# Feed-forward after attention without a barrier: first quarter from on-chip blocks, last head pair by quarters, layer 1 without a wait for stores

## The reference

```python
# layer 0; LN = (x - mean) / sqrt(var + 1e-5) over the 1024 features
x = x + 0.5 * ffn(LN(x))        # w1 (1024->4096), depthwise conv of 3 tokens, silu, w2 (4096->1024)
x = x + attn(LN(x))             # 16 heads of 64, softmax, W_o and bias
x = x + 0.5 * ffn(LN(x))        # the same weights a second time
# layer 1
x = x + 0.5 * moe(x); x = x + linear_attn(x); x = x + 0.5 * moe(x)
def bit_linear(x, w):           # in ffn: activations to int8 per token, weights to -1, 0, 1
    s = 127 / max(|x|, per token); return (round(x * s) / s) @ quant(w).T
```

## Time and profile before

| | us |
|---|---|
| time of the kernel, median of 3 runs | 3168.76 (3165.76 to 3183.69) |
| the profiled execution | 3179.94 |
| its span, first to last instruction of the slowest core (core 4) | 3178.4 |
| spans of the 8 cores | 3155.5 to 3178.4 |
| attention's last head pair | 1752 to 1838 |
| last value product to the first w1 product | 1838 to 1931 |
| first quarter of the second feed-forward | 1931 to 2065 |
| last w2 product to the first weight fusing in layer 1 | 2546 to 2571 |

### The profile page before, as it was taken

One profiled execution on the slowest core, in us unless ns is written; L12 is line 12 of the kernel. 1 busy time (PEld: TensorE's weight loads), 2 busy tenths in 40 slices (PEclk: granted clock), 3 DMA queues, 4 the chain that ended last, 5 costly groups with the idle time before them and its releaser, 6 DMA issues.

```text
span 3178.4 us, 39354 instructions; the slowest of 8 cores (3155.5 to 3178.4 us)
## 1 busy us (share of the span) xinstructions
PE 2623.4 (83%) x11770; PEld 1132.0 (36%) x11770; DVE 2017.5 (63%) x2898; ACT 1685.3 (53%) x1983; POOL 377.9 (12%) x438
## 2 busy tenths in 40 slices
PE   1558788895699999999988846697979879899899
PEld 0223233342233444444433312243434334344334
DVE  5698777763587777777767135877777324444443
ACT  5779666552326666666654725675655223414430
POOL 0000001213200110010010000011111212211310
PEclk6879899997899999999999977898989889999999
DMA  8656432335320321221061051142423550000002
GB/s 259 176 154 201 144 115 81 102 92 143 82 37 14 57 50 18 44 44 31 14 143 34 14 165 53 47 120 72 124 70 92 156 172 1 1 27 27 1 11 70
DMA packets 151756, 259.13 MB, mean 82 GB/s; under 512 B 35904, under 2 KB 71760, under 8 KB 151232
## 3 DMA queue, kind: packets, MB, share of 16 engines
q1 hardware_dynamic: 118832, 199.44, 21.5%
q0 software_dynamic: 32720, 57.17, 8.6%
HBM read 220.70 MB, written 52.56 MB: 86 GB/s over the span
## 4 chain that ended last, share of the span: by engine, by line
PE 64%; DVE 14%; ACT 9%; issue 8%; DMA 4%; POOL 1%; SPq 0%; DVEq 0%; ACTq 0%; POOLq 0%
PE fb L1731 11%; PE fb L1492 9%; PE aups L598 7%; PE mb L2316 7%; PE apps L712 6%; PE asps L693 6%; PE ajps L562 3%; PE mb L2107 2%; DVE amx L609 2%; PE rs L2205 2%; DVE fbig L1542 2%; PE mb L2373 2%; PE asps L657 2%; ACT fbig L1528 1%; PE st L2153 1%
## 5 line engine op out<-in xcount | busy, mean ns | idle before, releaser
L609 DVE TENSOR_REDUCE amx<-aups 128x1 f32<-128x512 f32 x1024 | 663.1, 687 | 213.0 <-PE aups L598 211.4
L702 ACT ACTIVATE aet<-asps 128x1024 bf16<-128x1024 f32 x512 | 523.1, 1024 | 279.6 <-PE asps L693 273.7
L1492 PE MATMUL fb<-shb,fw1r 128*128 128x512 bf16 x2048 | 542.6, 405 | 107.8 <-DVE fbig L1546 76.8
L1731 PE MATMUL fb<-fbig 128*128 128x512 bf16 x2048 | 494.5, 391 | 60.1 <-ACT fbig L1692 29.5
L598 PE MATMUL aups<-ahd 65*128 65x512 bf16 x1024 | 356.7, 386 | 21.2 <-DVE amx L609 8.3
L1492 PEld LDWEIGHTS fb<-shb,fw1r 128*128 128x128 fp8e4 x2048 | 207.5, 103 | 398.1 <-issue 198.9
L712 PE MATMUL apps<-aet,avt 128*65 128x512 bf16 x1024 | 311.6, 385 | 11.4 <-ACT aet L702 8.0
L1731 PEld LDWEIGHTS fb<-fbig 128*128 128x128 fp8e4 x2048 | 203.4, 100 | 320.7 <-issue 96.8
L693 PE MATMUL asps<-ahd 65*128 65x512 bf16 x1024 | 311.3, 387 | 0.0
L1528 ACT ACTIVATE fbig<-fb,cbsb,cw2sb 128x512 f32<-128x512 f32 x256 | 196.1, 769 | 203.0 <-PE fb L1492 189.9
L1542 DVE SCALAR_TENSOR_TENSOR fbig<-fb,cw2sb,fbig 128x511 f32<-128x511 f32 x256 | 191.2, 747 | 166.1 <-ACT fbig L1528 163.6
(11 more groups left out here) (280 smaller groups left out, 3073.7 us busy)
## 6 DMA issues: line engine op xcount, KB each, us to landing
fw1r<-wq SPq DMA_DIRECT2D x224, 128.0 KB, 2.2
fbig<-wq SPq DMA_DIRECT2D x112, 256.0 KB, 2.9
fbig<-w1h SPq DMA_DIRECT2D x32, 512.0 KB, 13.1
fbig<-w2h SPq DMA_DIRECT2D x28, 512.0 KB, 4.2
sha<-x SPq DMA_DIRECT2D x8, 1024.0 KB, 10.5
fw2f<-w2h SPq DMA_DIRECT2D x32, 256.0 KB, 3.8
fbig<-w2h SPq DMA_DIRECT2D x32, 256.0 KB, 3.8
fbig<-x POOLq DMA_DIRECT2D x32, 256.0 KB, 5.2
```

What stands on the lines that cost most here:

```text
L609: lambda e, hh=hh, c=c: e.tensor_reduce(m[:, c:c + 1], ups[hh][:, :], axis=AX.X, op=ALU.max),
L702: ta = A(lambda e: e.activation(et[g % 3][:, :], sps[s][:, :], AF.Exp, scale=0.125), wait=[tp, tk.get(("ef", g % 3))])
L1492: tp = T(lambda e, dc=dc: e.matmul(bank[b][:, :], sl[:, o + dc * 128:o + (dc + 1) * 128], xr[:, dc * 512:(dc + 1) * 512], start=(dc == 0), ...
L1731: tp = T(lambda e, j=j: e.matmul(bank[2 + j][:, :], w2r[s][:, o + j * 128:o + (j + 1) * 128], xi2[:, hc * 512:(hc + 1) * 512], start=(hc = ...
```

## The change

Three parts. (1) The last head pair goes by quarters: head 0 and head 1 of a quarter follow each other, so each quarter of the attention is complete after 16 steps. Its softmax sums no longer go through DRAM: a matmul with a 0/1 matrix `sel` spreads them over 128 partitions, DVE inverts 128x512 and multiplies. The remaining `g_wo` matmuls of pair 7 are done by step 39, and the rest (`g_rest`, pairs 5 to 7 of W_o) is pulled two a step from step 40 on. Stores go by the POOL queue. (2) The second feed-forward has no barrier. It takes quarter 0 where it lies (`xq` = `res[0..7]`), copies the halo columns from the blocks with DVE (`edge_copy`), and pulls the remaining blocks of `g_rest` between its layer norm's steps; the halo's steps lie between those of the quantisation. Reads of x from DRAM wait for the stores of their quarter only. (3) `layer1` waits for the compute engines' own counts instead of the barrier; its loads of x wait for the stores they need. Tiles are allocated in another order, so that none that is written early lies on one still in use.

```diff
@@ attn_l0
-                s_res = [dsem("ares") for _ in range(32)]
+                s_so = [dsem("aso") for _ in range(4)]
+                s_a7 = [[dsem("aa7") for _ in range(2)] for _ in range(2)]
+                s_res = [dsem("ares") for _ in range(16)]
-                def seq(g):
+                def seq(t, g):
+                    if t == 7:
+                        return (g // 8) % 2, g // 16, g % 8
                     return g // 32, (g // 8) % 4, g % 8
+                def last_pair(hh, qb, ta):
+                    base = hh * 64
+                    c = slice(qb * 512, (qb + 1) * 512)
+                    o = ao[:, 7 * T + qb * 512:7 * T + (qb + 1) * 512]
+                    r = rbc[1][:, c]
+                    tk["ao7", qb, hh] = dget(s_a7[qb % 2][hh],
+                        ao[base:base + 64, 7 * T + qb * 512:7 * T + (qb + 1) * 512],
+                        stg[hh][0:64, c],
+                        wait=[ta, tk["xln", 3], tk.get(("n7", qb - 2))])
...
+                    def inv():
+                        for h in range(2):
+                            tp = P(lambda e, h=h: e.matmul(
+                                ups[0][:, :], sel[:, h * 128:(h + 1) * 128],
+                                stg[h][0:65, c], start=(h == 0), stop=(h == 1)),
+                                wait=[tk["st7", qb, h], tk["u0f"],
+                                      tk["sel"]], mark=(h == 1))
+                        tk["u0f"] = tk["r7"] = V(
+                            lambda e: e.reciprocal(r, ups[0][:, :]),
+                            wait=[tp, tk["norm", 5]])
+                    def norm():
+                        tk["n7", qb] = V(lambda e: e.tensor_tensor(o, o, r, ALU.mult),
+                            wait=[tk["r7"], tk["ao7", qb, 0], tk["ao7", qb, 1]])
+                    after(1, inv)
+                    after(3, norm)
+                def g_rest():          # pulled from step 40 on, and in the next stage
...
+                            for ec in range(EA, DC):
+                                tp = wo_mm(rings[i], n, ec, EA, DC - 1, ...)
...
+                            t = V(lambda e, i=i, n=n: e.tensor_tensor(
+                                res[n], rings[i], res[n], ALU.add),
+                                wait=[tp, tk["res", n]])
+                            rt[i] = fin[n] = t
+                            out[qb] = dget(s_so[qb], x_dst[...], res[n],
+                                           wait=[t], eng="gpsimd")
-                        elif t == 7 or g >= 12:
-                            pull(p, 2 if t == 6 else 1)
+                        elif t == 6:
+                            pull(p, 2 if g >= 12 else 0)
+                        elif g < 40:
+                            pull(p, 2 if g % 5 < 2 else 1)
+                        else:
...
+                            pull(rest, 2)
@@ ffn
-            if not first:
-                barrier()
+            if prev is not None:
+                for e in ("scalar", "vector", "gpsimd", "sync"):
+                    em.wait_only(e, [prev["tk"]["pv", 7]])
+                def edge_copy(qb):
+                    t = None
+                    for d0, n, blk in prev["blocks"](qb):
+                        for b, o, c in ((qb, 0, 510), (qb - 1, 2, 0)):
+                            if b not in (0, 1, 2):
+                                continue
+                            t = V(... tensor_copy of two columns of n blocks ...,
+                                  wait=[prev["fin"][8 * qb + 7]])
-                    ln_load(0)
-                    for n in range(NW1):
-                        w1_load(n)
-                    ln_cast(0)
... (all steps of the layer norm, then halo(), then the quantisation)
+                    for n in range(NW1):
+                        w1_load(n)
+                    for k in range(4):
+                        w2_load(k)
+                    ln["dma"] = [fin[7], fin[7]]
+                    ln["held"] = [out[0]]
+                    edge_copy(0)
+                    steps = ln_steps(0)[1:]
+                    for k in range(13):
+                        steps.pop(0)()
+                        for _ in range(3):
+                            next(tail, None)
+                    for _ in tail:
+                        pass
+                    edge_steps = halo()
+                    for k in range(2):
+                        next(edge_steps)
+                    while steps:
+                        steps.pop(0)()
+                        for _ in range(2):
+                            next(edge_steps, None)
@@ layer1
-            barrier()
+            own = [(Sdv, Sdv.c), (Ssc, Ssc.c), (Spe, Spe.c)]
+            for e in ("tensor", "scalar", "vector"):
+                em.wait_only(e, own)
+            for e in ("gpsimd", "sync"):
+                em.wait_only(e, own + [(Sgp, Sgp.c)])
@@ layer1, x_load
-                                 wait=[tk.get(("out", q - 3))])
+                                 wait=[tk.get(("out", q - 3))] +
+                                 stored["x", q])
```

More of the change, by code:

```diff
@@ L478, in attn_l0 @@
                             k65[b][hh][64:65, :], 1.0))
+                V(lambda e: e.memset(sel[:, :], 0.0))
+                V(lambda e: e.memset(sel[64:65, 0:64], 1.0),
+                  wait=[(Sdv, Sdv.c)])
+                tk["sel"] = V(lambda e: e.memset(sel[64:65, 192:256], 1.0))
                 def ln_load(q):
@@ L760, in inv @@
                         if hh == 1:
-                            after(18 if t < 7 else 4, norm)
+                            after(18, norm)
                     def norm():
@@ L769, in norm @@
                                   tk["ao", t, 0], tk["ao", t, 1]])
-                    after(18 if t < 7 else 5, inv)
+                    after(18, inv)
                 EA = 5
@@ L863, in attn_l0 @@
                     tick()
-                    if t == 7:
-                        for _ in p:
-                            pass
                     if t == 5:
@@ L894, in attn_l0 @@
[L894 to L908 removed]
+                while 7 not in fin:
+                    pull(rest)
@@ new lines, in tail, with blocks, f @@
+                def tail():
+                    while later:
+                        pull(rest, 3)
+                        tick()
+                        yield
+                    for _ in rest:
+                        yield
+                def blocks(qb):
+                    def f(ap, n):
+                        return ap.rearrange("p (a b) -> p a b", a=n)
+                    if qb == 0:
+                        return [(0, 8, f(lnb[:, :], 8))]
+                    if qb < 3:
+                        o = (qb - 1) * 8192
+                        return [(0, 8, f(xln[:, o:o + 8192].bitcast(F32),
+                                         8))]
+                    return [(0, 4, f(qkb[:, :].bitcast(F32), 4))] + \
+                        [(4 + 2 * i, 2, f(wqk[i][:, :].bitcast(F32), 2))
+                         for i in range(2)]
@@ L910, in build_program, with ffn @@
+                return dict(tail=tail(), blocks=blocks, fin=fin, out=out,
+                            rt=rt, tk=tk)
         NW1 = 7
         stored = {}
-        def ffn(x_src, x_dst, first):
-            if not first:
-                barrier()
+        def ffn(x_src, x_dst, first, prev=None):
+            if prev is not None:
+                for e in ("scalar", "vector", "gpsimd", "sync"):
+                    em.wait_only(e, [prev["tk"]["pv", 7]])
             with ExitStack() as fctx:
@@ L1018, in ln_load, with made @@
                             .rearrange("(a p) t -> p a t", p=128),
-                            wait=[ln["xqfree"]]))
+                            wait=[ln["xqfree"]] + made(q)))
+                def made(q):
+                    return [prev["out"][q]] if prev is not None else []
                 def ln_cast(r):
@@ L1063, in ln_c @@
                         c, c, bc4(m_sb, 0, 512, 2), ALU.subtract),
-                        wait=[ln["m"]])
+                        wait=[ln["m"]] + ln.pop("held", []))
                 def ln_abs(r):
@@ L1527, in w1_item @@
                         old = old + [wtok["b", 30], wtok["b", 31]]
+                    if prev is not None and q == 0:
+                        old = [prev["tk"]["wo end"]]
+                        if hc >= 24:
+                            old += [prev["out"][i] for i in range(4)]
                     ta = A(lambda e: e.activation(
```

174 lines of the change are left out of this document (98 added, 76 removed).

## The result

The changed kernel takes 3130.1, 3132.8 and 3138.5 us (median 3132.8); the kernel before, on the same chip, has a median of 3171.9 us in four runs. The ratio is 0.9868, 95% interval 0.9822 to 0.9913: 42 us less (28 to 56). A second set gave 0.9856 (0.9829 to 0.9883). Some runs in which the cores of one die showed a much lower clock than those of the other (3338 us and the like) are left out of all comparisons here. Forecast were 3126 us and a gain of 42.5.

The account below looks back on a forecast made before the run. Dead time at the hand-over from attention to the second feed-forward and at its closing barrier was taken as the bound. Gains of 28 and 14.5 us sum to 42.5: 3168.8 becomes 3126 us, range 3103 to 3146.

Parts of the forecast that it names:

- The hand-over's wait: Last value product to layer norm's first cast: only ACT's copy remains, 53.2 us become 0.7, minus 52.5.
- Rival (d): Second feed-forward's start still held until the last store, only layer 1 gains: 3155 us; chance 0.06.
- The last pair, plus 18: Last head pair grows by 8 (products), 1.7 (`sel`), 6 (step 32) and 2 (step 47), about 18 us (8 to 25).
- The collision: Last pair, step 32: two inversions queue behind pair 6's `norm`; PE stands 4 us, then runs slower; together 6 us.
- `sel` and step 47: Last pair: 8 `sel` products, 1.7 us; at step 47 `inv` waits for ACT's copy, evictions behind the reciprocal, 2 us.
- The clock behind a pause: Last pair after step 32: PE at the lower clock level for some 6 us, 2.3 us more.
- rival (c): Clock falls in the last pair and stays low, pair 158 us: whole slower, 3185 to 3195 us; chance 0.03.
- The layer norm, plus 6.5: Quarter 0: evictions before largest absolute value plus 3.7, halo work behind transposes plus 5.1, halo off the chain minus 2.3.
- The barrier, 19.8: Head of layer 1: replacing the barrier by waits for engines' own counts gains 19.8 us.
- Layer 1's rest: Layer 1's start: plus 4.2, minus 6 for PE's pause for x, minus 3.5 for lower clock; net with barrier 14.5.
- Rival (a): Last pair has more slack, layer norm grows 3.5, products cost 0.08 each: gain 55.5, about 3110 us; chance 0.21.
- Rival (b): Layer 1's x lands after 15.1 us, layer norm's chain grows 12: gain 28, 3141 us; chance 0.17.

Follow-up runs that it names:

- experiment 4: Changed kernel with the last pair's inversions spaced, each fired right behind an eviction of the first W_o half's single bank: 3121.93 us.
- experiment 6: Changed kernel with the first W_o half's groups in the last pair alternating between two PSUM banks instead of one: 3126.34 us.
- experiment 7: Changed kernel with six instead of three W_o products between the first five steps of quarter 0's layer norm: 3132.07 us.
- experiment 10: Changed kernel with spaced inversions, two banks, later layer-1 statistics, more early layer-norm products: ratio to kernel before 0.9828; changed kernel again beside it: 0.9856.
- experiment 3: Changed kernel with the last pair's inversions and normalisations in a list of their own, quarters 0 to 2 inverting one step later: 3128.05 us.
- experiment 2: Changed kernel with the barrier put back at the head of layer 1: 3146.4 us (median of three), ratio to the kernel before 0.9914.

## Why the prediction was right

Direction, size and mechanism held; the whole came out at 3130 to 3139 for 3126. That the runs' 42 us (28 to 56) so nearly meet the 42.5 is partly luck: by stages the gain is 50. Step by step:

- **The hand-over's wait.** Forecast minus 52.5; measured 52.6 to 0.5 in the mean of the cores. What ended it was ACT's copy, no DMA. Rival (d) fell with it. The cover of the store held: quarter 0's last store is issued 27 us before the first centring (29 forecast) and lands 24 us before it.
- **The last pair, plus 18.** Measured 16.5 to 16.8. The sum was right, its terms partly by luck. The collision: forecast 6, measured 6.15 by its removal (experiment 4), with the pause at 3.61 for 4. The products: forecast 8 for 48, measured 5.6 (0.12 each instead of 0.16). `sel` and step 47, 1.7 and 2: not measured apart. What I had left out is that "those of `g_wo` are the same 56" are the same in number and not in place: finished by step 40, often two in a step, which cost 5.3 us in the first four eighths, 3.9 of it through the one bank (experiment 6), and some 0.9 in the fifth. The last three took back 1.5: 30.6 us before, with 16 of these products, and 29.2 with none (experiment 7).
- **The clock behind a pause.** Forecast some 6 us at the lower level after the collision, at a price of 2.3; the rows show 4.6 (1803.7 to 1808.3), and the collision's 6.15 less its pause leave 2.5. It came back within the pair, so rival (c) did not happen, though on some cores a 1.07 us wait for a bank did lower it for 3.4 us (experiment 10).
- **The layer norm, plus 6.5.** Measured 3.6 (to the first w1 product 3.3). Its three terms: 3.7 forecast and 2.9 measured; 5.1 and 4.0; minus 2.3 and minus 3.2. Each erred to the pessimistic side by about 1. In the first, DVE's waits for ACT shrank by 0.4 while the evictions came in, which a sum of DVE's instructions leaves out; the other two were not taken apart.
- **The barrier, 19.8.** Measured 19.7, on all cores.
- **Layer 1's rest.** Forecast minus 4.2 + 6 + 3.5 = plus 5.3; measured plus 4.5 in the mean. The sum is right and the terms are not. The pause was 4.3 at most instead of 6. The 4.2 for the clock did not come: I had called the pause, which is 2.4 us, too short to lower it, and the first 10.2 us of layer 1 ran at 0.67. This is the step that was wrong in kind. It also explains the shorter pause in part: at the lower level the four groups took 9.35 us instead of 7, so PE came later to its wait for x. The two errors hid each other.
- **Rival (a)** came true in part: the layer norm grew by 3.6 (3.5 in the rival) and a product cost 0.12 (between its 0.08 and my 0.16), but the collision cost its full price. The 50 us by stages lie between my 42.5 and its 55.5, and the runs' interval holds both.
- **Rival (b)** was not seen: x landed in time for ACT to start at 2524.89, 7.1 us after its issue at 2517.78 (5.8 forecast).
- **The sum.** Stages: 16.6 longer, 52.2 shorter, 3.3 longer, 2.6 shorter (the feed-forward itself, which was forecast unchanged and varies by some 10 us between cores), 19.7 shorter, 4.5 longer: 50, beside 53.1 by mean spans and 49.8 by the profiled executions. The ratio of the runs makes 42 and their medians differ by 39, since the profiled execution before was one of the longer ones and that after the shortest. Why layer 1 alone gave 10 us in the runs and 15 by its stages is open; the intervals don't exclude 14.6.

## What to carry to other kernels

When work moves into a stage, look for the long instruction of the engine that evicts: what costs is not its 3.4 us but the PSUM bank whose release stands behind it, and issuing it right behind an eviction made it free here. Work that keeps its number can still cost when it is issued in other steps, here two products at once on one bank. A barrier between stages can be dear even after the last store has landed (here 6.9 to 8.6 us of TensorE), so wait for the few counters that the next stage needs.

## What was new of the hardware

- TensorE's pause of 1.07 us in the first eighth of the pair was followed by products at full speed on some cores and by 3.4 us at the lower of the two levels on others (experiment 10); one of 1.89 us (experiment 3) by 3.4 us at it (a group of two 1.06 instead of 0.60 us), one of 3.61 us by 4.6 us, and one of 2.4 us between the layers by a granted clock of 0.67 over 10.2 us. What decides it for the shortest is not shown here. A short pause can cost more behind it than itself.
- With a barrier over all counters PE started 11.8 and SP 6.0 us after the last engine's work had ended, the same on every core although the last store landed after 3.2 to 4.8 us (experiment 2); with a wait for three counters PE started 0.36 us after the last eviction.
- The reciprocal of 128x512 takes 3.36 us from PSUM, as from SBUF.
